# Cross-attention and FP4 feed-forward, 64 sequences on one core: the residual of the output projection put into PSUM by ScalarE, on an accumulation that TensorE opened

## What is computed

```python
x = x + attention(layernorm(x), ctx, ctx, Wq, bq, Wout, bout)
x = x + ffn(layernorm(x), w_gate, w_up, w_down)

def attention(Q, K, V, Wq, bq, Wout, bout):
    q, k, v = (Q @ Wq + bq), (K @ Wq + bq), (V @ Wq + bq)     # 16 columns each
    corr = mean over all sequences and columns of the circular correlation of q and k
    W, I = softmax(top 12 of corr), their shifts
    R = sum over the 12 of W * roll(v, -I)                      # then repeated for 16 heads
    return R @ Wout + bout

def fp4_linear(x, w):     # both rounded to the FP4 grid, blocks of 16, scale = max/6
    return fp4(x) @ fp4(w).T

def ffn(x, w_gate, w_up, w_down):
    h = silu(fp4_linear(x, w_gate)) * fp4_linear(x, w_up)
    return fp4_linear(h, w_down)
```

## Time and profile before

| what | us |
|---|---|
| median of 3 runs | 478.52 |
| lowest, highest | 478.27, 481.03 |
| the profiled execution, device time | 479.78 |
| span of its trace | 477.3 |
| TensorE busy, VectorE busy | 445.2, 436.4 |
| ScalarE busy, GpSimd busy | 384.4, 248.5 |

### The profile page before, as it was taken

One profiled execution on the slowest core, in us unless ns is written; L12 is line 12 of the kernel. 1 busy time (PEld: TensorE's weight loads), 2 busy tenths in 40 slices (PEclk: granted clock), 3 DMA queues, 4 the chain that ended last, 5 costly groups with the idle time before them and its releaser, 6 DMA issues.

```text
span 477.3 us, 9868 instructions
## 1 busy us (share of the span) xinstructions
PE 445.2 (93%) x3362; PEld 300.8 (63%) x3362; DVE 436.4 (91%) x768; ACT 384.4 (81%) x642; POOL 248.5 (52%) x338
## 2 busy tenths in 40 slices
PE   4599995978699999999999999999999999999987
PEld 4488885844366666666666666666666666666675
DVE  3699987579999999999999999999999999999982
ACT  3369969599988888888888888888888888867572
POOL 4157750544466655665555666666666655433310
PEclk9799997999999999999999999999999999999999
DMA  7999901442256678656567666676666666555565
GB/s 242 339 349 347 345 13 33 90 90 67 59 116 138 139 121 159 128 126 129 129 130 139 140 134 139 132 134 131 139 139 137 140 116 141 107 105 106 119 139 129
DMA packets 164849, 68.66 MB, mean 144 GB/s; under 512 B 129216, under 2 KB 164544, under 8 KB 164800
## 3 DMA queue, kind: packets, MB, share of 16 engines
q1 hardware_dynamic: 164800, 68.03, 62.2%
HBM read 27.38 MB, written 9.18 MB: 77 GB/s over the span
## 4 chain that ended last, share of the span: by engine, by line
PE 80%; DVE 9%; ACT 3%; DMA 3%; issue 2%; SPq 1%; POOL 1%; DVEq 0%; POOLq 0%; ACTq 0%
PE ps L889 16%; PE ps L890 15%; PE ps L891 15%; PE ps L899 15%; PE ps L901 8%; PE ps L903 3%; PE ps L740 2%; PE ps L750 2%; DMA ctx_sb<-in_ctx_dram 2%; PE ps L763 2%; DVE a_bst L994 1%; ACT h_c L565 1%; DMA hqT<-ctx_sb 1%; ACT h_c L562 1%; DVE hb L1145 1%
## 5 line engine op out<-in xcount | busy, mean ns | idle before, releaser
L889 PE MATMUL ps<-guT_hi,a_xT 128*128 128x512 f16 (+1 forms) x384 | 139.5, 363 | 7.9 <-DVE hb L1145 5.4
L890 PE MATMUL ps<-guT_lo,a_xT 128*128 128x512 f16 (+1 forms) x384 | 139.5, 363 | 0.0
L891 PE MATMUL ps<-guT_hi,a_xT 128*128 128x512 f16 (+1 forms) x384 | 139.4, 363 | 0.0
L899 PE MATMUL ps<-dT_hi,hqT 128*128 128x256 f16 x704 | 129.2, 273 | 2.6 <-DMA hqT<-ctx_sb 2.6
L901 PE MATMUL ps<-dT_lo,hqT 128*128 128x256 f16 x384 | 87.3, 273 | 0.0
L492 POOL TENSOR_TENSOR ctx_sb<-w_q_lo,sl 128x704 f16<-128x704 f16 x58 | 87.2, 1524 | 0.0
L621 ACT ACTIVATE w_raw<-ps,inv_gu 128x704 f32<-128x704 f32 x64 | 53.9, 841 | 33.4 <-PE ps L891 33.3
L899 PEld LDWEIGHTS ps<-dT_hi,hqT 128*128 128x128 f16 x704 | 68.9, 98 | 13.7 <-DMA hqT<-ctx_sb 3.7
L508 POOL TENSOR_TENSOR sl<-bm,sh 128x240 f16<-128x240 f32 (+2 forms) x34 | 20.5, 604 | 95.0 <-DVE y_h L1241 72.8
L889 PEld LDWEIGHTS ps<-guT_hi,a_xT 128*128 128x128 f16 x384 | 37.7, 98 | 45.8 <-DMA a_xT<-ctx_sb 8.6
L562 ACT ACTIVATE h_c<-y_h 128x1408 bf16<-128x1408 bf16 (+3 forms) x39 | 47.9, 1227 | 20.1 <-DVE y_h L1241 16.6
(11 more groups left out here) (164 smaller groups left out, 794.9 us busy)
## 6 DMA issues: line engine op xcount, KB each, us to landing
xs<-in_x_dram SPq DMA_DIRECT2D x16, 512.0 KB, 8.4
ctx_sb<-in_ctx_dram SPq DMA_DIRECT2D x16, 512.0 KB, 7.9
out_dram<-a_xT SPq DMA_DIRECT2D x64, 128.0 KB, 2.2
w_raw<-a_scratch SPq DMA_DIRECT2D x60, 128.5 KB, 2.7
hqT<-ctx_sb SPq DMA_TRANSPOSE x64, 3.8
w_raw<-in_L_ffn_w_down_dram SPq DMA_DIRECT2D x1, 704.0 KB, 8.3
w_raw<-in_L_ffn_w_gate_dram SPq DMA_DIRECT2D x1, 640.0 KB, 5.0
w_raw<-in_L_ffn_w_up_dram SPq DMA_DIRECT2D x1, 640.0 KB, 6.3
```

Source lines behind the costliest of these rows:

```text
L889: pe.matmul(dst, xt[:, c, :], guT[0][:, c, n0:n1], start=(c == 0), stop=False)
L890: pe.matmul(dst, xt[:, c, :], guT[1][:, c, n0:n1], start=False, stop=False)
L891: last = pe.matmul(dst, xt[:, KC + c, :], guT[0][:, c, n0:n1], start=False, stop=(c == KC - 1))
L899: last = pe.matmul(dst, hqT[:, j % 4, c, :], dT_hi[:, c, :], start=(c == 0), stop=(added(j) and c == DCH - 1))
```

## The change

1. Which tiles: VectorE's evacuation (added) is now for the tiles 1, 5, 9, ... 53 alone (i mod 4 = 1), 14 of them where there were 28. A new predicate preset takes all other tiles from 2 to 55, 41 of them: the 27 even ones, which had the fp32 matmul, and the 14 tiles 3, 7, ... 55, which VectorE had evacuated.
2. For a preset tile TensorE issues one fp16 matmul early, ident16 x dT_hi with start=True (open_down), between gate_and_up(2n) and gate_and_up(2n+1), for the tiles 2n-6 and 2n-5. Its product is not used. It waits until the bank has been emptied of the tile two before (out_ready), by ScalarE or by VectorE.
3. ScalarE then overwrites the bank with xs * out_fac (preset_x), tile 2n-6 right after silu(2n), tile 2n-5 right after silu(2n+1), that is ahead of split_h.
4. The down product waits for that (o_set) and sums on it with start=False; it has no fp32 matmul any more.
5. ScalarE's evacuation of an odd tile stands before silu(2n) now (it stood after normalise_x, where in the steps 4 to 31 it did nothing before). VectorE's call is skipped in odd steps of n from 5 on.

The tiles 0 and 56 to 63 keep the fp32 matmul (9, where there were 36).

```diff
         def added(i):
-            return i % 2 == 1 and i // 2 < NP - 4
+            return i % 4 == 1 and i // 2 < NP - 4
+
+        def preset(i):
+            return i >= 2 and i % 4 != 1 and i // 2 < NP - 4
+
+        def n_added(i):
+            return (min(i, 2 * (NP - 4) - 1) + 3) // 4
+
+        def n_preset(i):
+            return i + 1 - 1 - n_added(i)
...
+            def preset_x(i):
+                if preset(i):
+                    act.wait_ge(s["o_open"], n_preset(i))
+                    act.activation(bank(6 + i % 2)[:, 0:D], xs[:, i, :], ACT.Copy, scale=out_fac[:, 0:1]).then_inc(s["o_set"], 1)
...
                     scale_high(st)
+                    residuals(2 * st - 7)
                     silu(2 * st)
+                    preset_x(2 * st - 6)
...
                     normalise_x(st + 3)
-                    residuals(2 * st - 7)
                     silu(2 * st + 1)
+                    preset_x(2 * st - 5)
                     split_h(j)
...
-                out_ready(pe, j - 2)
+                if preset(j):
+                    pe.wait_ge(s["o_set"], n_preset(j))
+                else:
+                    out_ready(pe, j - 2)
+                alone = added(j) or preset(j)
...
+            def open_down(j):
+                if preset(j):
+                    out_ready(pe, j - 2)
+                    pe.matmul(bank(6 + j % 2)[:, 0:D], ident16[:, :], dT_hi[:, 0, :], start=True, stop=False).then_inc(s["o_open"], 1)
+
...
+                    if n >= 4:
+                        open_down(2 * n - 6)
+                        open_down(2 * n - 5)
                     gate_and_up(2 * n + 1)
...
-                    if pair_ok(st - 4):
+                    if tile_ok(2 * st - 7) and added(2 * st - 7):
                         residual(2 * st - 7)
```

More of the change, by code:

```diff
@@ L207, in build @@
             "x1_done", "sq_done", "pool_st", "xn_ready", "x_max", "sc_steps", "sh_done", "sl", "x_split", "yx_done", "x4_steps",
-            "h_steps", "h_split", "yh_done", "h4_steps", "loh", "z_lo", "z_scale", "z_sh", "z_sl", "z_y", "z_split", "z_grid", "z_done", "o_done", "o_add", "id_out",
+            "h_steps", "h_split", "yh_done", "h4_steps", "loh", "z_lo", "z_scale", "z_sh", "z_sl", "z_y", "z_split", "z_grid", "z_done", "o_done", "o_add", "o_open", "o_set", "id_out",
             "hT0", "hT1", "hT2", "hT3", "xT0", "xT1", "gate_done", "gu_done", "sil_done", "d_done")}
@@ L262, in added @@
         def added(i):
-            return i % 2 == 1 and i // 2 < NP - 4
+            return i % 4 == 1 and i // 2 < NP - 4
[5 more added lines that the diff above has]
+            return i + 1 - 1 - n_added(i)
         def out_ready(eng, i):
             if added(i):
-                eng.wait_ge(s["o_add"], i // 2 + 1)
+                eng.wait_ge(s["o_add"], n_added(i))
             elif i >= 0:
-                eng.wait_ge(s["o_done"], i // 2 + 1 if i < 2 * (NP - 4) else i + 1 - (NP - 4))
+                eng.wait_ge(s["o_done"], i + 1 - n_added(i))
         def scaled(st):
@@ L896, in down @@
                 pe.wait_ge(hT[j % 4], 16 * (j // 4 + 1))
-                out_ready(pe, j - 2)
+                if preset(j):
[3 more added lines that the diff above has]
+                alone = added(j) or preset(j)
                 for c in range(DCH):
-                    last = pe.matmul(dst, hqT[:, j % 4, c, :], dT_hi[:, c, :], start=(c == 0), stop=(added(j) and c == DCH - 1))
+                    last = pe.matmul(dst, hqT[:, j % 4, c, :], dT_hi[:, c, :], start=(c == 0 and not preset(j)),
+                                     stop=(alone and c == DCH - 1))
                     if c < LOCH:
                         pe.matmul(dst, hqT[:, j % 4, c, :], dT_lo[:, c, :], start=False, stop=False)
-                if not added(j):
+                if not alone:
                     last = pe.matmul(dst, ident_out[:, :], xs[:, j, :], start=False, stop=True)
```

## The result

The changed kernel takes 486.37 us (median of 4 runs, 486.02 to 486.91), the kernel before 478.48 us beside it. The ratio is 1.0154, with a 95% interval of 1.0118 to 1.0189: slower by 1.5%; the medians are 7.9 us apart.

A forecast was written before the change was run, and what follows sets the result against it. TensorE and VectorE were both taken to set the pace, VectorE at 11.30 us a step. TensorE's gain and VectorE's residuals counted nothing; 14 x 0.68 = 9.5 us of lateness on 478.52 gave 488.0 us, range 480.0 to 492.8.

The forecast's parts named there:

- What bounds: Feed-forward steps: TensorE and VectorE both set the pace, VectorE at 11.30 us a step; ScalarE's hand-over has 0.44 us slack.
- TensorE's removed matmuls: TensorE: 27 fp32 matmuls removed, 41 fp16 ones added, net 7.1 us of its own time, turning into idle time.
- VectorE's removed residuals, costed at nothing: VectorE: 14 residuals of 0.40 removed, 5.6 us, all going into waiting for GpSimd's sum; gain taken as 0.
- The rule of the Trainium skill: Moving work from a saturated VectorE to ScalarE can pay; by it the residuals' 5.6 us come through.
- nothing in VectorE's next step takes this back: VectorE's odd step without a residual was still to take 11.30 us, so the 0.68 us lateness stays.
- x = 0.40: ScalarE's time per preset, an activation from SBUF into PSUM, taken as 0.40 us with ends 0 and 0.50.
- The estimate of 0.36: ScalarE's time per preset if PSUM access takes 51 ns against 93; the sum would be 0.6 us smaller.
- The moved wait: TensorE's second opening in even steps waits for VectorE's residual, making VectorE's next offset_h 0.68 us late (15.35 against 14.67).
- The count: The 0.68 us lateness was counted in 14 even steps (n = 4 to 30), 9.5 us in all.
- TensorE's account: Rival: TensorE binds, VectorE only follows, the opening's wait is covered; 7.1 us come off to 471.4; chance 0.11.
- The shorter VectorE step: Rival: odd steps without a residual become 0.40 shorter, two steps lose 0.28 net, 3.9 us, 482.4; chance 0.08.
- The case of the lower clock: Rival: waits drop TensorE's clock, over 1 us more per even step, above 502; chance 0.07 with other larger stalls.

The follow-up runs named there:

- e3: Changed kernel with VectorE keeping the residual of all odd tiles up to 55 and presets for the 27 even tiles only: 478.37 us against 479.43 before the change.
- e1: Changed kernel with the opening matmul of tile 2n-5 behind gate_and_up(2n+1) instead of ahead of it: 479.52 us against 479.43 before the change.
- e4: Late second opening behind gate_and_up(2n+1), plus GpSimd's sum cut to 32 of 256 columns from step 1 on: 471.83 us against 479.43 before the change.
- e7: Changed kernel with VectorE's residual before offset_h instead of after grid_x: 481.78 us against 479.27 before the change.
- e2: Changed kernel with ScalarE's preset of tile 2n-5 ahead of silu(2n+1) instead of behind it: 482.73 us against 479.43 before the change.
- e5: Kernel before with only TensorE's wait for VectorE's residual of tile 2n-7 moved ahead of gate_and_up(2n+1), no preset or opening: 483.36 us against 479.27.

## Why the prediction was right

**What bounds.** Right. VectorE's 11.30 us set the pace; e3 shows that TensorE's time was worth nothing up to step 31 (and 1.3 us in step 32), e1 the same in the steady steps with the full change.

**TensorE's removed matmuls.** As worked out: busy time fell, and the gain went into idle time at the second opening, 307.21 - 305.92 - 0.11 = 1.18 us in an even step, where I had written 1.2 (the 1.01 in brackets starts at the modelled end of the opening before, 0.16 later).

**VectorE's removed residuals, costed at nothing.** Right in eleven of the fourteen steps: 0.88 for 0.47 in step 19, and e4 and e7 confirm from both sides that GpSimd's sum takes it. In the steps 27, 29 and 31 it isn't, and this supports the reason: from step 27 on the sum has run out (step n sums pair n+5, and the last pair is 31). VectorE's product of step 27 in the changed kernel:

```profile
404.14 1.79 DVE L1174 SCALAR_TENSOR_TENSOR hb<-ps,h_in,w_raw 128x704 f32<-128x704 f32 x2
...
408.09 0.89 DVE L974 TENSOR_TENSOR h_t<-h_c,h_t 128x1408 f16<-128x1408 bf16 x1 [0.50 <-ACT h_c L574]
...
412.17 0.36 DVE L1179 TENSOR_TENSOR ctx_sb<-x_c,sh 128x512 f16<-128x512 f16 x1
...
415.51 1.80 DVE L1174 SCALAR_TENSOR_TENSOR hb<-ps,h_in,w_raw 128x704 f32<-128x704 f32 x2
```

The product takes 0.36. The step takes 11.37, only 0.19 more than before (11.18, with the residual still there and no sum either): VectorE is late by the same 0.6 and gets 0.40 back. The rule of the Trainium skill that I had set against the rows (Perfetto Trace Analysis, Optimizing Scalar/DVE Operations) holds in this trace where GpSimd's sum is absent, and "nothing in VectorE's next step takes this back" fails there.

**ScalarE's preset.** x = 0.40 was right: 310.86 to 311.26, and e2 returns 0.40 a pair of steps. The group of presets has a mean of 470 ns, between the two rows I bounded it by. The estimate of 0.36 from the Trainium skill's access figures (Perfetto Trace Analysis, Optimizing Scalar/DVE Operations) isn't borne out: with PSUM as the target the distance to the next start is 0.40, as for the square that writes SBUF. The square is another function, and no row shows the same copy from SBUF to SBUF, so this isn't a test of that figure alone.

**The moved wait.** Right in place and order, a little too large: I had 0.14 us from VectorE's end to TensorE's next start, and it took 307.21 - 307.15 = 0.06. This is the term that was mis-sized. It makes the lateness 0.60 where I had 0.68.

**The count.** 14 was too many. Eleven odd steps (5 to 25) took 11.90 instead of 11.30: 6.5 us. Steps 27 and 29 gave 0.2 and 0.3 only, for the reason just shown, and the steps 30 to 32 about 0.6 together (step 31 is 0.9 longer, step 32 is 0.4 shorter). The sum is 7.6 us against 7.9 between the medians; I had 9.5. So the size was overestimated by a fifth: the release makes 14 x 0.08 = 1.1 us of it, and the steps 27 and 29, which I hadn't looked at one by one, 0.7. The 1.3 us of TensorE's saving that e3 gains at the end I hadn't looked for either.

**The rivals.** TensorE's account fell with e3. The shorter VectorE step fell with e7 and the odd steps. That the preset or its PSUM writes cost time by themselves fell with e1. The case of the lower clock didn't come either: the granted clock stands at 1.00 in the window above and over 150 to 440 us as a whole, the upper of its two levels, in spite of an idle 1.2 us in every other step.

## What to carry to other kernels

When two engines are busy for 40 of 40 us, the page's chain can't tell which binds: compare what one step takes where an instruction is absent, or lighten one engine and see which one shows idle time. A wait that is moved up in a queue is paid by what is queued behind it; follow it to the next hand-over and compare with that hand-over's slack (here 0.44 us), not with an engine's idle share. And put a cheap opening instruction that waits for another engine behind the work that doesn't need it: e1 is the same change without the loss.

## What the runs showed that I had not expected

GpSimd's sum slows VectorE's product even in the steps where a residual fills the time: 0.47 with it, 0.36 without (e4), 0.11 us a step. By an estimate from that, 23 x 0.11 for the steps 4 to 26, about 2.5 us of the kernel before are this wait, and the steps 1 to 3, at 0.87, have 0.5 each besides.

The end of the program doesn't follow the steady steps. The last steps (27 to 32) have less work for VectorE and no sum on GpSimd, and what follows them takes under 20 us. e5 lost 4.1 us where its steady steps explain 2.0, e7 lost 2.5 where they explain 4.3, and e3 gained its 1.3 in step 32 alone. A forecast by steady steps alone misses it.
